# Four graph layers on one core: the node work behind the GCN and GGN edge stages put between their last 48 visits

## What is computed

```
x = layernorm(x + GAT(x))       # two attention layers
x = layernorm(x + GCN(x))
x = layernorm(x + relation_attention(x))
x = layernorm(x + GGN(x))       # result
```

```
GCN:  dis = rsqrt(degree); out = segment_sum((x @ W)[src] * dis[src] * w * dis[dst], dst) + b
GGN:  h = x @ W_in.T + b_in; agg = segment_sum((h @ W_msg)[src], dst)
      r, z, n = gates(agg @ W_ih.T, h @ W_hh.T); h_new = (1 - z) * n + z * h
      out = h_new @ W_out.T + b_out
```

## Time and profile before

| | us |
|---|---|
| median of 3 runs | 5875.3 (5874.98 to 5880.74) |
| profiled execution | 5873.96 |
| its span, first to last instruction | 5872.1 |
| GCN edge stage, first gather to last add | 2219.1 to 3211.4 |
| node phase between GCN and the relation layer | 3211.4 to 3298.9 |
| GGN edge stage, first gather to last add | 4783.1 to 5770.4 |
| gates, norm and stores at the end | 5770.4 to 5872.1 |

### The profile page before, as it was taken

How to read it: one execution, slowest core, us unless ns; L and a number is a source line. 1 busy time by engine, 2 the same in 40 slices (tenths; PEclk the granted TensorE clock), 3 DMA queues, 4 the chain that set the end, 5 groups by cost and what they waited for, 6 DMA issues and landing times. The chain is left out here.

```text
span 5872.1 us, 104159 instructions
## 1 busy us (share of the span) xinstructions
PE 3565.8 (61%) x29228; PEld 3190.6 (54%) x29332; DVE 3613.2 (62%) x11040; ACT 1534.2 (26%) x3908; POOL 3981.7 (68%) x4360
## 2 busy tenths in 40 slices
PE   4666466566466654455565688888866864444456
PEld 3555455555355553444554577787755753344444
DVE  4699566799544464444554788888879952223335
ACT  0477000577100020000000455555540140000004
POOL 6777777377777737777776577777742457777772
PEclk8555788755555575555555899999988975555558
DMA  6688444488433326677771477777745722222221
GB/s 174 188 242 238 132 128 126 143 242 242 122 87 84 86 81 157 168 175 182 190 198 47 153 211 211 210 212 212 212 135 150 205 65 53 53 53 53 53 53 37
DMA packets 511398, 846.19 MB, mean 144 GB/s; under 512 B 116566, under 2 KB 220655, under 8 KB 510271
## 3 DMA queue, kind: packets, MB, share of 16 engines
q0 software_dynamic: 140576, 316.92, 22.0%
q1 hardware_dynamic: 210451, 305.33, 16.3%
q10 hardware_dynamic: 159840, 217.27, 13.1%
HBM read 654.62 MB, written 186.50 MB: 143 GB/s over the span
## 5 line engine op out<-in xcount | busy, mean ns | idle before, releaser
L2453 POOL DMA_INDIRECT s_rows<-rel_tab,src_v x832 | 787.0, 946 | 270.8 <-issue 250.8
L265 POOL DMA_INDIRECT gcn_rows<-gcn_tab,src_g x784 | 747.7, 954 | 247.9 <-issue 229.6
L265 POOL DMA_INDIRECT stash<-gat_tab,src_g x784 | 752.1, 959 | 239.6 <-issue 151.7
L265 POOL DMA_INDIRECT ggn_rows<-ggn_tab,src_g x784 | 742.8, 947 | 246.9 <-issue 238.3
L1621 PE MATMUL e_psb<-tmp,e_oh 128*128 x3328 | 654.7, 366 | 409.4 <-DVE e_oh L1589 355.3
L265 POOL DMA_INDIRECT stash<-in_x,src_g x732 | 707.9, 967 | 225.0 <-issue 145.5
L1621 PEld LDWEIGHTS e_psb<-tmp,e_oh 128*128 128x128 f32 x3328 | 581.6, 264 | 482.9 <-issue 482.5
L2124 PE MATMUL gcn_pso<-gcn_rows,gcn_oh 128*128 x1952 | 493.2, 434 | 481.8 <-SPq L970 439.3
L1953 PE MATMUL ggn_pso<-ggn_rows,ggn_oh 128*128 x1952 | 449.2, 410 | 507.4 <-SPq L970 505.9
L1953 PEld LDWEIGHTS ggn_pso<-ggn_rows,ggn_oh 128*128 128x128 f32 x1952 | 397.9, 306 | 559.3 <-issue 559.3
L2124 PEld LDWEIGHTS gcn_pso<-gcn_rows,gcn_oh 128*128 128x128 f32 x1952 | 426.9, 323 | 505.2 <-issue 505.2
(11 more groups left out here) (507 smaller groups left out, 8187.4 us busy)
## 6 DMA issues: line engine op xcount, KB each, us to landing
g_lo_rows<-lo_rows ACTq DMA_DIRECT2D x392, 256.0 KB
oh_dram<-tmp ACTq DMA_DIRECT2D x208, 256.0 KB, 3.4
s_oh<-oh_dram SPq DMA_DIRECT2D x208, 256.0 KB
edge_v<-acc SPq DMA_DIRECT2D x208, 256.0 KB, 2.8
r_values<-edge_v SPq DMA_DIRECT2D x208, 256.0 KB, 3.0
edge_v<-stash SPq DMA_DIRECT2D x205, 256.0 KB, 3.9
e_values<-edge_v SPq DMA_DIRECT2D x205, 256.0 KB, 2.7
tmp<-drel_rows ACTq DMA_DIRECT2D x208, 128.0 KB
```

The lines of the kernel that those rows point to most:

```text
L265: pool.indirect_dma_start(rows[:, t, :], None, tab[:, :], bass.IndirectOffsetOnAxis(ap=edges[:, t:t + 1], axis=0)).then_inc(s_land, 16)
L2453: pool.indirect_dma_start(rows[:, n % RING, t, :], None, rel_tab[:, :], bass.IndirectOffsetOnAxis(ap=src_v[:, n * GT + t:n * GT + t + 1], ...
```

## The change

Both node phases are dissolved into the edge stages before them. The blocks are cut into 13 parts instead of quads: part 0 is block 0, part q the four blocks 4q - 3 to 4q. Part q is begun right after visit 196 + 4q in GCN (its blocks are complete by then) and 197 + 4q in GGN, and its steps are spread over the following visits, by a number of visits that each step has been given on its engine. Part 12 begins behind the last visit, so a rest of the work stands behind the loop of visits.

```diff
 RC = VT // VR
 BANKS = 4
 WIDTH = P * TC
+NODE_PARTS = tuple([(max(0, 4 * q - 3), 4 * q + 1) for q in range((BLOCKS + 3) // 4)])
+STATIC_V = 188
+GATE_AT = GROUPS + 1
+GATE_PARTS = tuple([(max(0, 4 * q - 3), 4 * q + 1) for q in range((BLOCKS + 3) // 4)])
+NORM_FIRST = len(GATE_PARTS) - 3
+NORM_CUT = GATE_PARTS[NORM_FIRST][0]
 
...
                     def _(pool):
                         pool.sem_inc(s_o, RING)
                         gather_rows(pool, rows, ggn_tab, s_row, s_o)
+                        pool.wait_ge(s_r, 2)
+                        for b in range(NORM_CUT):
+                            xb = x_n[:, b * D:(b + 1) * D]
+                            nc.gpsimd.tensor_scalar(xb, xb, sd[:, b:b + 1], off[:, b:b + 1], ALU.mult, ALU.add).then_inc(s_y[0], 1)
+                        pool.wait_ge(s_r, 4)
+                        for b in range(*TAIL[0]):
+                            xb = x_n[:, b * D:(b + 1) * D]
+                            nc.gpsimd.tensor_scalar(xb, xb, sd[:, b:b + 1], off[:, b:b + 1], ALU.mult, ALU.add).then_inc(s_y[1], 1)
...
+                        for first, last in GATE_PARTS[:NORM_FIRST]:
+                            sp.wait_ge(s_y[0], last)
+                            store(first, last)
+                        for i, (first, last) in enumerate(TAIL):
+                            sp.wait_ge(s_y[i + 1], last - first)
+                            store(first, last)
+                        sp.wait_ge(s_done, 16 * (len(GATE_PARTS) + 1))
```

```diff
+                        def gate(v):
+
+                            if part(v, 2) is not None:
+                                new_gate(part(v, 2))
+                            if part(v, 3) is not None:
+                                hidden(part(v, 3))
+                            if part(v, 5) is not None:
+                                put(part(v, 5))
+                            if part(v, 7) == NORM_FIRST - 1:
+                                scales(0, 0, NORM_CUT)
...
                         def body(v, k):
                             front(v + 1, k + 1)
                             back(v, k)
+                            gate(v)
...
                         back(V - 1, (V - 1) % RING)
-                        dve.wait_ge(s_acc, V + 2)
+                        for v in range(V - 1, GATE_AT + 4 * LAST_PART + 6):
+                            gate(v)
+                        scales(1, NORM_CUT, BLOCKS)
+                        dve.wait_ge(s_r, 4)
+                        for b in range(*TAIL[1]):
+                            xb = x_n[:, b * D:(b + 1) * D]
+                            v_.tensor_scalar(xb, xb, sd[:, b:b + 1], off[:, b:b + 1], ALU.mult, ALU.add).then_inc(s_y[2], 1)
```

```diff
+                        for q in range(LAST_PART + 1):
+                            w = wid(q)
...
+                            if q >= 1:
+                                squares(q - 1)
+                            if q == NORM_FIRST:
+                                deviations(0, NORM_CUT, NORM_FIRST)
+                            act.wait_ge(s_n, q + 1)
+                            f(nn[:, 0:w], nn[:, 0:w], ACT.Tanh, bias=b_ih[:, 2:3]).then_inc(s_t, 1)
+                        squares(LAST_PART)
+                        deviations(NORM_CUT, BLOCKS, LAST_PART + 1)
+                        act.wait_ge(s_r, 4)
+                        for b in range(*TAIL[2]):
+                            xb = x_n[:, b * D:(b + 1) * D]
+                            f(xb, xb, ACT.Identity, scale=sd[:, b:b + 1], bias=off[:, b:b + 1]).then_inc(s_y[3], 1)
...
+                        def gate(v):
+
+                            if part(v, 0) is not None:
+                                turn(part(v, 0))
+                                state(part(v, 0))
+                            if part(v, 1) is not None:
+                                gates(part(v, 1))
+                            if part(v, 4) is not None:
+                                output(part(v, 4))
```

```diff
+            def part(v, d):
+
+                q, r = divmod(v - GROUPS - d, 4)
+                return q if r == 0 and 0 <= q < len(NODE_PARTS) else None
+
+            def statics(v):
+
+                first, stop = [min(ITERS, -(-w * ITERS // STATIC_V)) for w in (v, v + 1)]
+                return range(first, stop)
+
+            LAST_PART = len(NODE_PARTS) - 1
+            END = GROUPS + 4 * LAST_PART
             with phase() as st:
                 rows = sb(st, "gcn_rows", [P, SLOTS, GT, D])
                 oh = sb(st, "gcn_oh", [P, 2, GT, P])
...
+                        def normed(q):
+                            first, last = NODE_PARTS[q]
+                            act.wait_ge(s_sc, 2 * q + 2)
+                            for b in range(first, last):
+                                xb = x_n[:, b * D:(b + 1) * D]
+                                m = f(xb, xb, ACT.Identity, scale=sd[:, b:b + 1], bias=off[:, b:b + 1])
+                            m.then_inc(s_x, 1)
+                            act.wait_ge(s_x, q + 1)
+                            act.dma_start(rel_tab[first * P:last * P, 0:D].rearrange("(b p) d -> p b d", p=P),
+                                          x_n[:, first * D:last * D].rearrange("p (b d) -> p b d", d=D)).then_inc(s_sx, 16)
...
+                        def taken(q):
+                            first, last = NODE_PARTS[q]
+                            act.wait_ge(s_evd, q + 1)
+                            act.dma_start(rel_tab[first * P:last * P, D:2 * D].rearrange("(b p) d -> p b d", p=P),
+                                          gsb[:, q % 2, 0:last - first, :]).then_inc(s_st[q % 2], 16)
+                            act.wait_ge(s_ch, q + 1)
+                            f(q_part(0, q), rest[:, 0:last - first, :], ACT.Copy).then_inc(s_q0, 1)
+
+                        deviation(0)
+                        normed(0)
+                        for q in range(1, LAST_PART + 1):
+                            turned(q - 1)
+                            deviation(q)
+                            normed(q)
+                            taken(q - 1)
+                        turned(LAST_PART)
+                        taken(LAST_PART)
```

```diff
+                        def node(n):
+                            if n == STATIC_V + 2:
+                                mask()
+                            if n == STATIC_V + 4:
+                                mask_end()
+                                for k in range(RING):
+                                    dve.wait_ge(s_ost[k], ITERS // RING * 16)
+                                dve.wait_ge(s_nv, ITERS)
+                                dve.wait_ge(s_tm, 4)
+                            if part(n, 0) is not None:
+                                sums(part(n, 0))
+                            if part(n, 5) is not None:
+                                take(part(n, 5))
+                            if part(n, 6) is not None:
+                                pieces(part(n, 6))
+                            if part(n, 1) is not None:
+                                scales(part(n, 1))
+
+                        for n in range(V - 1):
+                            if n % RING == 0 and 1 <= n // RING <= QUADS:
+                                add_bias(v, b_gcn, n // RING - 1)
+                            for i in statics(n):
+                                static(i)
                             body(n, n % RING)
+                            node(n)
...
+                        for n in range(V - 1, END + 7):
+                            node(n)
...
+                        def node(n):
+                            if part(n, 3) is not None:
+                                turn(part(n, 3))
+                            if part(n, 4) is not None:
+                                products(part(n, 4))
+
...
-        with ExitStack() as spare:
-            rest = sb(spare, "q_rest", [P, 2, 4, D])
-            s_r1 = top.enter_context(nc.semaphore("q_pieces"))
-            norm_nodes("reln", gcn_in, w_xq[:, :, :].rearrange("p a d -> p (a d)"), 2 * D,
-                       [(rel_tab[:, 0:D], x_n), (rel_tab[:, D:2 * D], None)], rel_take_act, rel_take_dve)
...
-        ggn_gates()
```

512 lines of the change are left out of this document (268 added, 244 removed).

## The result

The changed kernel took 5739.0 us (median of 4 runs, 5735.2 to 5742.7), the kernel before 5875.1 beside it (4 runs). The ratio is 0.977, 95% interval 0.975 to 0.978: 136 us less, for a forecast of 5741.

The account below looks back on a forecast made before the run. POOL's gather issue was taken to bound the edge stages, with node phases standing behind them. Gains 67.5 - 4 + 70.7 - 0 = 134.2 us off 5873.96 gave 5739.8, 5741 with the median's 1.3 more; range 5724 to 5782.

Parts of the forecast that it names:

- What bounds the edge stages: Both edge stages run at the pace of POOL's gather issue, 1.26 us each; no compute engine is the limit.
- GCN's tail: Node work left behind GCN's last add, up to the next gather: 20 us in place of 87.5.
- the lower end: GCN's node work behind the last add takes 16.5 us if eight product matmuls run in 1.89 us, not 3.62.
- GCN's lag: Delay of GCN's visits by node work queued between them: 4 us.
- The clock: PE's granted clock in the stretches with visits and node work together: 0.75 expected, from 0.52 and 0.61.
- the first rival: PE stays at the lower clock beside the gathers; GCN lags 20 us, GGN 56; time 5813; chance 0.16.
- GGN's tail: Node work left behind GGN's last add, up to the end of the span: 31 us in place of 101.7.
- GGN's lag: Delay of GGN's visits by gates between them: 0, since PE's 155 us of work is under 164.7.
- the third rival: Gathers slow down beside DVE work, 0.96 to 1.56 us each, 152 us in all; time 5893; chance 0.02.
- POOL's normalization: POOL's 41 blocks behind GGN's last gather take 21 to 23 us, well within the 31 behind the last add.
- The static steps: 208 one-hot builds in 188 visits, 20 visits with a second one, cost nothing; at most 40 us without cover.
- The serial rival: Queues run the parts one after the other: 22.3 us a part in GCN, 25.4 in GGN; time 5978; chance 0.03.

Follow-up runs that it names:

- all_behind: Changed kernel with all parts begun behind the last visit, in the new order, so without overlap with the visits: 5942.3 us, ratio 1.0115 to the kernel before.
- the two halves: Two kernels, each with only one stage changed (GCN or GGN) and the other as in the kernel before: 5808.9 us each, ratios 0.989 and 0.9885.
- zn_in_psum: Changed kernel with the tanh of z and the candidate n of GGN's gates kept in PSUM: 5739.9 us.
- beside_wide: Changed kernel plus useless 512-column DVE steps, two a visit, in GGN's visits 124 to 193, with inputs varied: 5764.8 us.
- gcn_in_place: Changed kernel with all steps of a GCN part asked for in place behind the visit that begins it: 5831.0 us.

## Why the prediction was right, and where it was not

- *What bounds the edge stages.* Right. POOL did not wait for PE (the 7.3 us, 9.1 before, are its usual gaps), and the last gathers came at nearly the same distance from the first. `all_behind` and the two halves show that the overlap is the gain.
- *GCN's tail.* 20 us forecast with 16.5 as the lower end, 17.2 measured, but not for the reason that the lower end had: the clock was 0.60 and the products ran at the slow rate. The chain from the first sum to the last store was 12.1 us (3215.76 to 3227.89) where the old first quad's 15.5 had been taken. That quad's chain held a table load on ACT (1.28 us) and the next quad's transposes ahead of its products (1.1 us), and the new tail has neither. The store's issue to the next gather was 5.0 us (4.4 taken).
- *GCN's lag.* 4 us forecast, 4.5 measured between first gather and last add, of which 3.2 is the gathers' own distance, and that for more than half the spread of the runs. The waits named were the ones that came: in the last 48 visits DVE waited 17.8 us in nine parts for ACT's first piece. Gain of the stage 65.7 us (63.5 forecast).
- *The clock.* 0.75 expected, 0.79 and 0.83 measured in the last 48 visits (0.52 and 0.61 before), so the first rival did not come. PE's busy time times clock is 79 and 110 us there, where the prediction had summed 80 and 116. `all_behind` gives the other side: the same GCN work with gaps had 0.58.
- *GGN's tail.* 31 us forecast, 30.7 measured, and in the parts that were forecast: 16.4 us from the last add to the last part's first output (16.2), 14.3 from there to the end (14.8). POOL's 37 early blocks were over at 5724.2, 14 us behind the last add (17 forecast for all its blocks).
- *GGN's lag: the step that failed.* It was put at 0 because PE's work fits into the pace. It measured 5.2 us, and the gain of the half is 65.8 us instead of 70.7. The pace itself had changed: 5.6 us between first and last gather, which is the third rival in small. Five other runs with these gates show 983.6 to 984.5 us, three without any beside the visits 979.4 to 980.5, so 4 us is the steadier figure. Their last adds came 990.1 to 990.9 us behind the first gather, against 986.2 to 987.3 without: 4 us again. In `zn_in_psum` the gathers won most of this back and the last add did not, but there PE's products also wait for the mix; how much of the lag the gathers alone make in the changed kernel is not shown.
- *The evidence against that rival* was the wrong kind of DVE work. The prediction held the score stage against it, where DVE is busy for most of the time and gathers take 0.946 us. These are two of the longest steps that DVE does there, from the groups of the kernel before (busy us, mean ns, idle before):

```profile
L2482 DVE TENSOR_TENSOR s_psr<-s_psr,s_rows 128x512 f32<-128x512 f32 x207 | 144.7, 699 | 139.1 <-DMA s_rows<-rel_tab,src_v 136.9
L2507 DVE TENSOR_TENSOR tmp<-s_psk,tmp 128x512 f32<-128x512 f32 x205 | 141.2, 689 | 0.0
```

Each reads one tensor of PSUM (`s_psr`, `s_psk`) and one of SBUF, which `beside_wide` prices at 0.02 us a gather. Of the steps that moved beside GGN's gathers, four a part read two of SBUF, and all 14 gathers over 1.1 us in the last 48 visits of the changed profile run beside one of these. The rule of the Trainium skill that the prediction cited ("GPSIMD Engine Reference", section 8, Key points) spoke of two SBUF inputs, and the test should have been by inputs, not by busy share. The kernel before had such a case. GCN's longest gather there, the 2025 ns in the earlier trace rows, stands beside the time mask's additions of two SBUF tensors:

```profile
3085.49 1.30 DVE L2097 TENSOR_TENSOR tmp<-tmp 128x832 f32<-128x832 f32 x1
3085.59 2.02 POOL L265 DMA_INDIRECT gcn_rows<-gcn_tab,src_g  x1 [0.30 <-issue]
3086.83 1.30 DVE L2099 TENSOR_TENSOR tmp<-tmp 128x832 f32<-128x832 f32 x1
```

- *POOL's normalization.* With the mixes beside it 37 blocks took 19.4 us, 0.536 each; in `zn_in_psum`, where only the first mix of a part reads two SBUF tensors, 16.7, 0.462. DVE's state mixes in that tail (L1972, L1974) took 0.81 and 0.82 us in the mean instead of 0.69. No run varied this alone. Both held within the 31 us.
- *The static steps.* Costing nothing was right, also at 58 doubled visits.
- *The serial rival* was priced at 22.3 us a part; in `gcn_in_place` it took 21.8 us. Its effect on POOL was misjudged: POOL did not wait, and the lag stood behind the last gather.

The sum by the profiles is 65.7 + 65.8 = 131.5 us (134.2 forecast). The medians differ by 136.2; the 5 us between these lie within the spread of single executions. That the forecast of 5741 came within 2 us of the median is in part luck: by the profiles GCN's tail was put 2.8 us too long and GGN's lag 5.2 too short, and these partly cancel.

In GCN two of the piece steps of a part also read two SBUF tensors of 512 columns, and yet the mean gather of the last 48 visits is 0.962 us in both kernels. The means hide it: the one before holds the time mask with its 2.02 us gather, which the change moved out of this stretch. In `all_behind`, where neither stands there, it is 0.948. In the changed kernel the six longest gathers of the stretch (1.10 to 1.46 us) all run beside the piece steps:

```profile
3171.78 0.69 DVE L2443 TENSOR_TENSOR reln_rest<-reln_rest,acc 128x512 f32<-128x512 f32 x1 [2.03 <-ACT acc L2338]
3171.83 1.46 POOL L271 DMA_INDIRECT gcn_rows<-gcn_tab,src_g  x1 [0.30 <-issue]
```

Two things stay open: what sets the tails, and why steps with one SBUF input stretch the gathers a little.

## What to carry to other kernels

Where an issue queue sets the pace and the engines stand half idle, work of the next phase belongs between its last steps as soon as its inputs are complete; count what comes back as a tail, and spread each part's steps so that no engine asks for a result that was only just begun (worth 90 us in GCN). Steps that are good between other work can be worse standing alone, so judge the order in its place. Beside a queue of indirect gathers on POOL, look at the inputs of wide DVE steps, not at how busy DVE is, and look for what ends next before paying to move them.

## What the hardware showed that I had not expected

- An indirect gather's issue took 1.05 to 1.08 us instead of 0.944 in the mean beside 512-column DVE mixes with two SBUF inputs, single ones up to 1.9 us, and 0.966 with one input in PSUM; 128-column mixes left it at 0.950.
- It goes both ways: DVE's state mixes took up to 0.82 us instead of 0.69 beside POOL's arithmetic, and POOL's blocks 0.536 instead of 0.462.
- PE took in 50 us more of work in GGN's last 48 visits (132.6 us busy against 82.6) in 5 us more time, with the granted clock at 0.83 instead of 0.61.
